# The order of four instructions in the projection stage of a two-layer recurrent and attention model

## The chip, the core and the metric

The kernel is written in Bass for one core of a Trainium2 chip. The metric is the device time of one execution in microseconds (us), lower being better. The engines are called as in the profile: PE is TensorE, DVE is VectorE, ACT is ScalarE, POOL is GpSimd, SP is SyncE, which here issues the transfers. Each engine takes its instructions strictly in the order written, and waits where the code says `wait_ge`.

## What is computed

Two layers over x of shape (4, 2048, 256). Each is `x + s * silu(g)` on a layernorm of x. In layer 0, s is a recurrent mix over time and g a feed-forward net. In layer 1, s is a latent attention with rotary parts, and g is a channel mix. The stage of interest makes all operands of layer 1's attention and its gate. Of the reference:

```python
xn = _layernorm(x)
c_q = x @ W_DQ;  Qc = c_q @ W_UQ;  Qr = rope(c_q @ W_QR)
c_kv = x @ W_DKV;  Kc = c_kv @ W_UK;  Kr = rope(x @ W_KR);  V = c_kv @ W_UV
# gate: mixes of every row with the row before it
xr = mu_r * x + (1.0 - mu_r) * x_prev
xk = mu_k * x + (1.0 - mu_k) * x_prev
r = sigmoid(xr @ W_r.T)
out = r * (square(relu(xk @ W_k.T)) @ W_v.T);  g = silu(out)
```

In both halves the x is the normalised xn.

## The kernel before

Four stages follow each other: layer0, layer1_projections, attention, layer1_output. Each is a block with a barrier at its end. The stage of interest, layer1_projections (from L924), walks over 16 chunks of 512 tokens (4 batches of 4 chunks). Products are made in float16, with every operand as a high part (the value rounded) and a low part (the rest), so most tensors are made in two steps: X_high, a copy with rounding, mostly on ACT, then X_low = X - X_high on DVE or POOL.

The order is written out by hand: each engine has a function `body(b, c, left)` that issues its instructions for chunk n, and semaphores count the steps. `left` is 4 in the first three batches and then 3, 2, 1, 0, so `left >= 1` holds for chunks 0 to 14, and `left >= 2` for chunks 0 to 13. Work for the chunks ahead is woven in. In the order of the code the body for chunk n is, for each engine:

- PE (L1499 on): latents (lat), keys of the gate (k), key rotary part (kr); with the latents qc (L1484) and the query rotary part; the transposes of chunk n+1 (L1477, wait for xhat); then, when relu and xr_low are there, the first half of the products of xr with w_r, kc (waits for qc_low), the second half, the values, and the gate's value products (L1546), which wait for kc_low and act_k. All go through four PSUM tensors, two banks each.
- ACT (L1289 on): qc_high (L1293); xn_of(n+1) (L1231 to L1245), which reads the transposes and has kc_high (L1297) in its middle; sigmoid of r (L1304); values (L1307); xk_high(n+1) (L1254); qr_high (L1312); xr_high(n+1) (L1260); the latents of n+1 (L1280); normalise(n+2) (L1225, four activations, waits for rstd(n+2)); relu of n+1 (L1284); gate_sig (L1321).
- DVE (L1418 on): latents' low part, two key products with cosine and sine (L1430), qc_low (L1433), two query products (L1437), the layernorm statistics of n+2 (L1333), kc_low (L1442), aggregate(n+2) (L1340), xn_low(n+1) (L1345), mix(n+1) (L1354, xk and then xr), xk_low(n+1) (L1359), qr_low (L1452), gate_in (L1457).
- POOL (L1176 on): the key sum k_cos + k_sin (L1180); the square of relu (L1183); kr_high, a cast of 8x512 (L1186); the query sum (L1188); kr_low (L1190); rstd_of(n+2) (L1157 to L1162, four small instructions, waits for the aggregate of n+2); xr_low_of(n+1) (L1166, waits for xr_high of n+1); the gate product (L1198, waits for gate_sig).
- SP stores qc, kr, kc, qr, values and gate of each chunk, and loads rows four chunks ahead.

Of the kernel before, what the change touches and what calls it, by code (L numbers as in the profile page):

```python
# [10 lines left out]
ACT = mybir.ActivationFunctionType  # L11
# [8 lines left out]
TPC = CH // P  # L20
# [900 lines left out]
STORES = 5  # L921


def layer1_projections(nc, a, d, ident, rows_out, early, scales, first):  # L924
# [6 lines left out]
    with ExitStack() as ctx:  # L931
# [10 lines left out]
        relu = sb("b_relu", [P, KT, CH])  # L942
# [23 lines left out]
        scale = sb("b_scale", [P, ATTN + 1])  # L966
# [22 lines left out]
        k_cos = sb("b_kcos", [D_R, CH])  # L989
# [4 lines left out]
        kr = sb("b_kr", [D_R, 2, 2, CH], F16)  # L994
# [5 lines left out]
        ps_b = ctx.enter_context(nc.psum_tensor("b_ps1", [P, 2, CH], F32))  # L1000
# [7 lines left out]
        stored = [sem(f"b_stored{i}") for i in range(2)]  # L1008
# [8 lines left out]
        stats_done = sem("b_stats_done")  # L1017
# [16 lines left out]
        k_mm = sem("b_k_mm")  # L1034
# [6 lines left out]
        relu_done = sem("b_relu_done")  # L1041
# [6 lines left out]
        kr_sum = sem("b_kr_sum")  # L1048
        kr_high = sem("b_kr_high")
# [36 lines left out]
        def count(b, c):  # L1086

            return b * CPB + c

        def turns(b, c):  # L1090

            return b * (CPB // 2) + c // 2

        with nc.Block() as block:  # L1094
# [47 lines left out]
            @block.gpsimd  # L1142
            def _(pool):
                for counts_from_one in (kr_low, gate_done):
                    pool.sem_inc(counts_from_one, 1)
                pool.memset(half[:], -0.5).then_inc(consts_set, 1)
                pool.memset(zero_col[:], 0.0).then_inc(consts_set, 1)
                pool.memset(ones[:], 1.0).then_inc(consts_set, 1)
                pool.memset(eps[:], LN_EPS).then_inc(consts_set, 1)
                pool.memset(zeros[:], 0.0).then_inc(consts_set, 1)  # L1150
                pool.wait_ge(consts_set, 5)

                def rstd_of(n):

                    pool.wait_ge(mv_done, TPC * n + TPC)
                    pool.wait_ge(xhat_done, TPC * n)
                    nc.gpsimd.tensor_tensor(var_eps[:], mv[:, :, 1], eps[:], ALU.add).then_inc(rstd_done, 1)  # L1157
                    nc.gpsimd.tensor_tensor(shift[:], zeros[:], mv[:, :, 0], ALU.subtract).then_inc(rstd_done, 1)
                    pool.wait_ge(rstd_done, 4 * n + 2)
                    nc.gpsimd.tensor_tensor(rstd[:], var_eps[:], half[:], ALU.pow).then_inc(rstd_done, 1)  # L1160
                    pool.wait_ge(rstd_done, 4 * n + 3)
                    nc.gpsimd.tensor_tensor(shift[:], shift[:], rstd[:], ALU.mult).then_inc(rstd_done, 1)  # L1162

                def xr_low_of(n):
                    pool.wait_ge(xr_high, n + 1)
                    nc.gpsimd.tensor_tensor(xr_half[:, 1], x_r[:], xr_half[:, 0], ALU.subtract).then_inc(xr_low, 1)  # L1166

                rstd_of(0)
                rstd_of(1)
                xr_low_of(0)  # L1170
                pool.memset(val[:], 0.0).then_inc(consts_set, 1)
                pool.wait_ge(consts_set, 6)
                for s in range(2):
                    pool.memset(val[:, s].rearrange("p g j h e -> p (g j h) e")[:, :, D_H:D_H + 1], 1.0).then_inc(consts_set, 1)

                def body(b, c, left):  # L1176
                    n, s = count(b, c), c % 2

                    pool.wait_ge(kr_parts, 2 * n + 2)
                    nc.gpsimd.tensor_tensor(k_cos[:], k_cos[:], k_sin[:], ALU.add).then_inc(kr_sum, 1)  # L1180

                    pool.wait_ge(relu_done, n + 1)
                    nc.gpsimd.tensor_tensor(act_k[:], relu[:], relu[:], ALU.mult).then_inc(act_done, 1)  # L1183
                    pool.wait_ge(kr_sum, n + 1)
                    pool.wait_ge(stored[s], 16 * STORES * turns(b, c) + 16)
                    nc.gpsimd.tensor_copy(kr[:, s, 0, :], k_cos[:]).then_inc(kr_high, 1)  # L1186
                    pool.wait_ge(qr_parts, 2 * n + 2)
                    nc.gpsimd.tensor_tensor(q_cos[:], q_cos[:], q_sin[:], ALU.add).then_inc(qr_sum, 1)  # L1188
                    pool.wait_ge(kr_high, n + 1)
                    nc.gpsimd.tensor_tensor(kr[:, s, 1, :], k_cos[:], kr[:, s, 0, :], ALU.subtract).then_inc(kr_low, 1)  # L1190
                    if left >= 2:
                        rstd_of(n + 2)
                    if left >= 1:
                        xr_low_of(n + 1)

                        pool.wait_ge(gate_sig_done, n + 1)
                        pool.wait_ge(rows_out.stored[s], 16 * (NCH // 2 + turns(b, c)) + 16)
                        nc.gpsimd.tensor_tensor(gate[s][:], gate_in[:], gate_sig[:], ALU.mult).then_inc(gate_done, 1)  # L1198

                chunks(pool, body)  # L1200

            @block.scalar
            def _(act):
# [75 lines left out]
                        act.wait_ge(lat_mm, 2 * n + i + 1)  # L1279
                        nc.scalar.activation(lat[:, i], ps_a[:, i, :], ACT.Copy, scale=f).then_inc(lat_high, 1)  # L1280

                def mixed_keys(n):
                    act.wait_ge(k_mm, n + 1)
                    nc.scalar.activation(relu[:], ps_b[:], ACT.Relu, scale=mix_k_factor).then_inc(relu_done, 1)  # L1284

                latents_high(0)
                mixed_keys(0)

                def body(b, c, left):  # L1289
                    n, s = count(b, c), c % 2  # L1290
                    act.wait_ge(stored[s], 16 * STORES * turns(b, c) + 16)
                    act.wait_ge(qc_mm, n + 1)
                    nc.scalar.activation(qc[:, s, 0], ps_c[:], ACT.Copy, scale=q_factor).then_inc(qc_high, 1)  # L1293

                    def keys_high():
                        act.wait_ge(kc_mm, n + 1)
                        nc.scalar.activation(kc[:, s, 0], ps_c[:], ACT.Copy, scale=k_factor).then_inc(kc_high, 1)  # L1297

                    if left >= 1:
                        xn_of(n + 1, c + 1, keys_high)  # L1300
                    else:
                        keys_high()
                    act.wait_ge(r_mm, n + 1)
                    nc.scalar.activation(sig_r[:], ps_r, ACT.Sigmoid, scale=r_factor).then_inc(sig_done, 1)  # L1304
                    act.wait_ge(val_mm, n + 1)
                    act.wait_ge(consts_set, 8)
                    nc.scalar.activation(val[:, s, :, :, :, 0:D_H].rearrange("p g j h e -> p g (j h) e"),  # L1307
                                         ps_val.rearrange("p j (g h e) -> p g j h e", g=GROUPS, h=GH), ACT.Copy, scale=v_factor).then_inc(val_done, 1)
                    if left >= 1:
                        xk_high_of(n + 1)  # L1310
                    act.wait_ge(qr_sum, n + 1)
                    nc.scalar.activation(qr[:, s, 0, :], q_cos[:], ACT.Copy).then_inc(qr_high, 1)  # L1312
                    if left >= 1:
                        xr_high_of(n + 1)
                        latents_high(n + 1)
                    if left >= 2:
                        normalise(n + 2, c + 2)
                    if left >= 1:
                        mixed_keys(n + 1)
                    act.wait_ge(gate_in_done, n + 1 + 1)  # L1320
                    nc.scalar.activation(gate_sig[:], gate_in[:], ACT.Sigmoid).then_inc(gate_sig_done, 1)  # L1321

# [3 lines left out]
            def _(dve):  # L1326
# [8 lines left out]
                def aggregate(n):  # L1335

                    if n:
                        dve.wait_ge(rstd_done, 4 * n - 2)
                    for j in range(TPC):
                        nc.vector.bn_aggr(mv[:, j, :], stats[:, j, :]).then_inc(mv_done, 1)  # L1340
# [16 lines left out]
                def xk_low_of(n):  # L1357
                    dve.wait_ge(xk_high, n + 1)
                    nc.vector.tensor_tensor(xk_half[:, 1], x_k[:], xk_half[:, 0], ALU.subtract).then_inc(xk_low, 1)  # L1359
# [58 lines left out]
                def body(b, c, left):  # L1418
# [20 lines left out]
                    if left >= 2:  # L1439
# [1 line left out]
                    dve.wait_ge(kc_high, n + 1)  # L1441
                    nc.vector.scalar_tensor_tensor(kc[:, s, 1], ps_c[:], factor[:, WUK:WUK + 1], kc[:, s, 0],  # L1442
                                                   ALU.mult, ALU.subtract).then_inc(kc_low, 1)
                    if left >= 2:
                        dve.wait_ge(stats_done, TPC * (n + 2) + TPC)
                        aggregate(n + 2)
                    if left >= 1:
                        xn_low_of(n + 1)
                        mix(n + 1, c + 1)
                        xk_low_of(n + 1)  # L1450
                    dve.wait_ge(qr_high, n + 1)
                    nc.vector.tensor_tensor(qr[:, s, 1, :], q_cos[:], qr[:, s, 0, :], ALU.subtract).then_inc(qr_low, 1)  # L1452

# [637 lines left out]
```

## Time and profile before

| | us |
|---|---|
| median of 3 executions | 3606.49 |
| lowest, highest | 2026.82, 8032.47 |
| profiled execution | 2026.82 |
| its span, first to last instruction | 2025.1 |
| layer0, from 0 to 638.8 | 638.8 |
| layer1_projections, to 950.2 | 311.4 |
| attention, to 1962 | 1011.8 |
| layer1_output, to the end | 63.1 |

The profile is of one execution. A row of a timeline has the start in us from the span's start, the length, engine and line, the operation, output and inputs, and, after x, how many instructions it merges. In square brackets stands how long the engine was idle before it and what ended that. Of instructions that follow each other directly, the next may start up to 0.1 us before the end of the one before, so the distance of two starts (here called a slot) is what one costs.

### The profile page before, as it was taken

The page shows a single profiled execution, that of the slowest core. Times are in us where ns is not written, and L with a number is a line of the kernel's source. Part 1 is how long each engine was busy: PE and PEld are TensorE (multiplying, and loading weights), DVE is VectorE, ACT ScalarE, POOL GpSimd, SP SyncE. Part 2 cuts the span into 40 slices and gives each one's busy share as a digit, 9 for nine tenths or more (in the row PEclk, how much of TensorE's full clock was granted, in tenths as well). Part 3 has the DMA queues.
Part 4 walks back from the last instruction along what each step waited for, and adds up shares of the span by engine and source line. Part 5 has one row for each costly group of instructions (what it writes and reads, how often), then busy time and mean ns, then how long its engine had stood idle before and what let it go on. Part 6 is the DMA issues. An engine that isn't in the chain of part 4 may idle for free. (4 is left out here: it accounts for less than half of the span.)

```text
span 2025.1 us, 53401 instructions
## 1 busy us (share of the span) xinstructions
PE 1900.1 (94%) x22950; PEld 978.9 (48%) x22950; DVE 1729.8 (85%) x2249; ACT 1727.0 (85%) x2153; POOL 547.4 (27%) x426
## 2 busy tenths in 40 slices
PE   3999999999995999998999999999999999999986
PEld 1565565655653566664444443444434444344445
DVE  5999999999987788886888888888888888888878
ACT  5767867777666888886999999999999999999972
POOL 0564554655644666764000000000000000000004
PEclk9999999999997999998999999999999999999999
DMA  3001001001112356567221222222222222122129
GB/s 108 22 22 42 22 22 42 22 22 42 54 42 78 129 191 204 190 170 210 70 75 55 67 68 74 73 55 68 68 74 72 62 62 55 51 62 60 56 96 329
DMA packets 130220, 166.24 MB, mean 82 GB/s; under 512 B 13632, under 2 KB 101696, under 8 KB 129728
## 3 DMA queue, kind: packets, MB, share of 16 engines
q1 hardware_dynamic: 127952, 160.59, 26.5%
q8 instruction: 180, 2.95, 0.6%
q10 hardware_dynamic: 2032, 2.24, 0.3%
q14 instruction: 56, 0.46, 0.1%
HBM read 91.21 MB, written 71.57 MB: 80 GB/s over the span
## 5 line engine op out<-in xcount | busy, mean ns | idle before, releaser
L1757 ACT ACTIVATE c_probs<-c_ps_b 128x1536 f32<-128x1536 f32 x544 | 891.9, 1640 | 0.0
L1871 PE MATMUL c_ps_o<-c_probs,c_v 128*32 128x256 f32 (+3 forms) x6656 | 582.3, 453 | 3.9 <-DVE c_probs L1789 0.8
L1789 DVE TENSOR_SCALAR c_probs<-c_probs 128x2048 f32<-128x2048 f32 (+2 forms) x415 | 433.7, 1055 | 68.2 <-ACT c_probs L1757 67.8
L1851 PE MATMUL c_ps_b<-c_qk 24*128 24x256 f16 (+2 forms) x8064 | 459.9, 294 | 5.7 <-PEq L1094 5.7
L1851 PE MATMUL c_ps_a<-c_qk 24*128 24x256 f16 (+2 forms) x2688 | 449.9, 294 | 6.5 <-ACT c_probs L1756 4.9
L1756 ACT ACTIVATE c_probs<-c_ps_a 128x512 f32<-128x512 f32 x544 | 422.9, 777 | 2.5 <-PE c_ps_a L1851 2.4
L1851 PEld LDWEIGHTS c_ps_b<-c_qk 24*128 24x128 f16 x8064 | 222.8, 93 | 332.6 <-ACT c_probs L1757 243.9
L2022 POOL TENSOR_TENSOR d_prod<-d_prod,d_x 128x1024 f32<-128x1024 f32 x4 | 13.1, 3262 | 1029.4 <-DVE d_prod L2011 1029.4
L1871 PEld LDWEIGHTS c_ps_o<-c_probs,c_v 128*32 128x32 f32 x6656 | 161.7, 109 | 245.8 <-issue 126.9
L278 POOL TENSOR_TENSOR a_hidh<-a_hid,a_hidh 128x512 f16<-128x512 f32 x128 | 207.2, 1648 | 135.2 <-ACT a_hidh L404 134.0
L1794 DVE TENSOR_SCALAR c_probs<-c_probs 128x1536 f32<-128x1536 f32 (+2 forms) x208 | 165.6, 803 | 55.9 <-ACT c_probs L1757 53.6
L1851 PEld LDWEIGHTS c_ps_a<-c_qk 24*128 24x128 f16 x2688 | 199.3, 93 | 18.0 <-ACT c_probs L1756 15.3
L728 PE MATMUL a_ps<-a_xnh,a_w 128*128 128x512 f16 x768 | 176.2, 381 | 12.8 <-ACT a_hid L399 12.0
L728 PE MATMUL a_ps<-a_w,a_hidh 128*128 128x256 f16 x1536 | 170.8, 273 | 1.5 <-POOL a_hidh L278 1.5
L1798 DVE SCALAR_TENSOR_TENSOR c_probs<-c_probs,c_caps 128x512 f32<-128x512 f32 x256 | 169.5, 682 | 0.0
L728 PEld LDWEIGHTS a_ps<-a_w,a_hidh 128*128 128x128 f16 x1536 | 149.9, 98 | 23.3 <-POOL a_hidh L278 2.4
L728 PEld LDWEIGHTS a_ps<-a_xnh,a_w 128*128 128x128 f16 x768 | 72.1, 97 | 114.2 <-ACT a_hid L399 29.0
L399 ACT ACTIVATE a_hid<-a_ps,a_b 128x512 f32<-128x512 f32 x128 | 87.9, 687 | 20.2 <-PE a_ps L728 15.1
L728 PE MATMUL a_ps<-a_xnh,a_wr 128*128 128x512 f16 x384 | 87.1, 383 | 10.3 <-DVE a_wv L525 10.3
L477 ACT ACTIVATE a_rwkvh<-a_rwkv 128x1024 f16<-128x1024 f32 x16 | 16.9, 1057 | 79.1 <-DVE a_rwkv L693 79.1
L515 DVE TENSOR_TENSOR a_xmixh<-a_xmix,a_xmixh 128x1024 f16<-128x1024 f32 x32 | 77.3, 2453 | 0.0
L1764 DVE STREAM_TRANSPOSE c_otok<-c_ps_o 128x512 f32<-128x512 f32 x64 | 45.8, 716 | 35.2 <-PE c_ps_o L1871 35.2
(272 smaller groups left out, 2776.9 us busy)
## 6 DMA issues: line engine op xcount, KB each, us to landing
v_d<-b_val SPq DMA_DIRECT2D x16, 1024.0 KB
c_v<-v_d SPq DMA_DIRECT2D x64, 256.0 KB
rows<-in_x SPq DMA_DIRECT2D x16, 512.0 KB, 4.9
x_d<-rows_out SPq DMA_DIRECT2D x16, 512.0 KB, 3.3
rows<-x_d SPq DMA_DIRECT2D x16, 512.0 KB, 5.0
qc_d<-b_qc SPq DMA_DIRECT2D x16, 512.0 KB
kc_d<-b_kc SPq DMA_DIRECT2D x16, 512.0 KB
gate_d<-rows_out SPq DMA_DIRECT2D x16, 512.0 KB, 3.3
```

The costliest lines, as they stand in the source:

```text
L278: nc.gpsimd.tensor_tensor(hid_half[:, 1, m], hid[:, m % RING], hid_half[:, 0, m], ALU.subtract).then_inc(hid_low, 1)
L399: nc.scalar.activation(hid[:, m % RING, :], ps_a[:, m % 2, :], ACT.Relu, bias=b_1[:, m:m + 1], scale=hid_scale).then_inc(hid_done, 1)
L515: nc.vector.tensor_tensor(x_mix_half[i][:, 1], x_mix[m][:], x_mix_half[i][:, 0], ALU.subtract).then_inc(mix_low, 1)
L728: mm = nc.tensor.matmul(ps, l, r, start=(first and i == 0), stop=(last and i == len(steps) - 1))
L1756: nc.scalar.activation(probs[:, t % NPROB, PARTS[0]], ps_a[:], ACT.Exp, scale=unscale).then_inc(exp_a_done, 1)
L1757: nc.scalar.activation(probs[:, t % NPROB, PARTS[1]], ps_b[:, t % 2], ACT.Exp, scale=unscale).then_inc(exp_b_done, 1)
L1764: nc.vector.transpose(o_tok[:, e % 2].rearrange("p k r -> p (k r)"), ps_o[:]).then_inc(tok_done, 1)
L1789: nc.vector.tensor_scalar(tile, tile, P_MAX, P_MIN, ALU.min, ALU.max).then_inc(clip_done, 1)
L1794: nc.vector.tensor_scalar(tile[:, :, at:end], tile[:, :, at:end], P_MAX, P_MIN, ALU.min, ALU.max)
L1798: op = nc.vector.scalar_tensor_tensor(tile[:, :, at:at + P], tile[:, :, at:at + P], P_MIN, cap, ALU.max, ALU.min)
L1851: mm = nc.tensor.matmul(into, k[rows, hk, kt * P:(kt + 1) * P], tokens[rows, hq], start=(i == 0), stop=(i == len(TERMS) - 1), tile_positio ...
L1871: mm = nc.tensor.matmul(ps_o[j * VW:(j + 1) * VW, column:column + w], v[:, kt, j * VW:(j + 1) * VW], probs[:, step % NPROB, j, at:at + w], ...
```

## The change

It moves four instructions or groups within `layer1_projections`, all inside the bodies above. On POOL the cast kr_high goes away, and xr_low_of(n+1) is put in front of rstd_of(n+2) where it was behind it. On ACT the same cast is made as an ACTIVATE between xn_of(n+1) and the sigmoid of r, and the relu, which stood before gate_sig at the end of the body of the chunk before, is the first instruction of its own chunk's body, and so comes right behind gate_sig. On DVE aggregate(n+2) goes from before xn_low(n+1) to behind xk_low(n+1).

```diff
--- before.py
+++ after.py
@@ -1181,17 +1181,15 @@
 
                     pool.wait_ge(relu_done, n + 1)
                     nc.gpsimd.tensor_tensor(act_k[:], relu[:], relu[:], ALU.mult).then_inc(act_done, 1)
-                    pool.wait_ge(kr_sum, n + 1)
-                    pool.wait_ge(stored[s], 16 * STORES * turns(b, c) + 16)
-                    nc.gpsimd.tensor_copy(kr[:, s, 0, :], k_cos[:]).then_inc(kr_high, 1)
                     pool.wait_ge(qr_parts, 2 * n + 2)
                     nc.gpsimd.tensor_tensor(q_cos[:], q_cos[:], q_sin[:], ALU.add).then_inc(qr_sum, 1)
                     pool.wait_ge(kr_high, n + 1)
                     nc.gpsimd.tensor_tensor(kr[:, s, 1, :], k_cos[:], kr[:, s, 0, :], ALU.subtract).then_inc(kr_low, 1)
+                    if left >= 1:
+                        xr_low_of(n + 1)
                     if left >= 2:
                         rstd_of(n + 2)
                     if left >= 1:
-                        xr_low_of(n + 1)
 
                         pool.wait_ge(gate_sig_done, n + 1)
                         pool.wait_ge(rows_out.stored[s], 16 * (NCH // 2 + turns(b, c)) + 16)
@@ -1279,15 +1277,12 @@
                         act.wait_ge(lat_mm, 2 * n + i + 1)
                         nc.scalar.activation(lat[:, i], ps_a[:, i, :], ACT.Copy, scale=f).then_inc(lat_high, 1)
 
-                def mixed_keys(n):
+                latents_high(0)
+
+                def body(b, c, left):
+                    n, s = count(b, c), c % 2
                     act.wait_ge(k_mm, n + 1)
                     nc.scalar.activation(relu[:], ps_b[:], ACT.Relu, scale=mix_k_factor).then_inc(relu_done, 1)
-
-                latents_high(0)
-                mixed_keys(0)
-
-                def body(b, c, left):
-                    n, s = count(b, c), c % 2
                     act.wait_ge(stored[s], 16 * STORES * turns(b, c) + 16)
                     act.wait_ge(qc_mm, n + 1)
                     nc.scalar.activation(qc[:, s, 0], ps_c[:], ACT.Copy, scale=q_factor).then_inc(qc_high, 1)
@@ -1300,6 +1295,8 @@
                         xn_of(n + 1, c + 1, keys_high)
                     else:
                         keys_high()
+                    act.wait_ge(kr_sum, n + 1)
+                    nc.scalar.activation(kr[:, s, 0, :], k_cos[:], ACT.Copy).then_inc(kr_high, 1)
                     act.wait_ge(r_mm, n + 1)
                     nc.scalar.activation(sig_r[:], ps_r, ACT.Sigmoid, scale=r_factor).then_inc(sig_done, 1)
                     act.wait_ge(val_mm, n + 1)
@@ -1315,8 +1312,6 @@
                         latents_high(n + 1)
                     if left >= 2:
                         normalise(n + 2, c + 2)
-                    if left >= 1:
-                        mixed_keys(n + 1)
                     act.wait_ge(gate_in_done, n + 1 + 1)
                     nc.scalar.activation(gate_sig[:], gate_in[:], ACT.Sigmoid).then_inc(gate_sig_done, 1)
 
@@ -1441,13 +1436,13 @@
                     dve.wait_ge(kc_high, n + 1)
                     nc.vector.scalar_tensor_tensor(kc[:, s, 1], ps_c[:], factor[:, WUK:WUK + 1], kc[:, s, 0],
                                                    ALU.mult, ALU.subtract).then_inc(kc_low, 1)
-                    if left >= 2:
-                        dve.wait_ge(stats_done, TPC * (n + 2) + TPC)
-                        aggregate(n + 2)
                     if left >= 1:
                         xn_low_of(n + 1)
                         mix(n + 1, c + 1)
                         xk_low_of(n + 1)
+                    if left >= 2:
+                        dve.wait_ge(stats_done, TPC * (n + 2) + TPC)
+                        aggregate(n + 2)
                     dve.wait_ge(qr_high, n + 1)
                     nc.vector.tensor_tensor(qr[:, s, 1, :], q_cos[:], qr[:, s, 0, :], ALU.subtract).then_inc(qr_low, 1)
```

## Rows read from the trace of the kernel before

**Rows 1.** Windows: the stage; busy us (count) of PE, PEld, DVE, ACT, POOL; PE clock

```profile
638.80:950.20 311.40, 283.34 (x1570) 175.74 (x1570) 252.97 (x432) 247.47 (x356) 197.93 (x184) 0.96 0.60 189
```

**Rows 2.** Windows, same columns: one chunk, from one qc ACTIVATE to the next

```profile
756.79:774.61 17.82, 17.43 (x100) 10.88 (x99) 15.07 (x25) 14.83 (x21) 12.26 (x12) 1.00 0.59 192
```

**Rows 3.** Timeline of PE, 740 to 780: start, length, what [idle before <-releaser]

```profile
763.23 3.72 PE L1546 MATMUL b_ps<-b_wv,b_actk 128*128 128x256 f32 x16 [0.39 <-DVE b_kc L1442]
766.79 2.75 PE L1484 MATMUL b_ps<-b_xnh,b_wc 128*128 128x512 f16 x12
...
776.14 1.48 PE L1484 MATMUL b_ps<-b_wr,b_xrh 128*128 128x256 f16 x12
```

**Rows 4.** Waits of ten chunks, 703.35 to 881.50: us in total, times, longest

```profile
POOL b_xrh L1166 <- ACT b_xrh L1260: 21.8, 10, 2.2
```

**Rows 5.** Timeline of ACT, 755 to 780, columns as in rows 3

```profile
756.79 1.02 ACT L1293 ACTIVATE b_qc<-b_ps 128x1024 f16<-128x1024 f32 x1 [0.48 <-PE b_ps L1484]
...
760.83 1.02 ACT L1297 ACTIVATE b_kc<-b_ps 128x1024 f16<-128x1024 f32 x1
...
765.98 1.06 ACT L1254 ACTIVATE b_xkh<-b_xk 128x1024 f16<-128x1024 f32 x1 [1.14 <-DVE b_xk L1354]
766.94 0.61 ACT L1312 ACTIVATE b_qr<-b_qcos 128x512 f16<-128x512 f32 x1
767.46 1.04 ACT L1260 ACTIVATE b_xrh<-b_xr 128x1024 f16<-128x1024 f32 x1
...
770.07 2.06 ACT L1225 ACTIVATE b_xhat<-rows,b_shift,b_rstd 128x256 f32<-128x256 f32 x4
772.17 1.02 ACT L1284 ACTIVATE b_relu<-b_ps 128x1024 f32<-128x1024 f32 x1
773.09 1.05 ACT L1321 ACTIVATE b_gs<-b_gi 128x1024 f32<-128x1024 f32 x1
```

**Rows 6.** Timeline of DVE, 755 to 780

```profile
760.37 1.40 DVE L1333 BATCH_NORM_STATS2 b_stats<-rows 128x6 f32<-128x256 f32 x4
761.89 1.28 DVE L1442 SCALAR_TENSOR_TENSOR b_kc<-b_ps,b_factor,b_kc 128x1024 f16<-128x1024 f32 x1
763.09 0.37 DVE L1340 BATCH_NORM_AGGREGATE b_mv<-b_stats 128x2 f32<-128x6 f32 x4
763.38 1.25 DVE L1345 SCALAR_TENSOR_TENSOR b_xnh<-b_ps,b_scale,b_xnh 128x1024 f16<-128x1024 f32 x1
764.55 1.40 DVE L1354 SCALAR_TENSOR_TENSOR b_xk<-b_ps,b_mix_now,b_prev 128x512 f32<-128x512 f32 x2
```

**Rows 7.** Timeline of POOL, 755 to 780

```profile
764.68 0.19 POOL L1157 TENSOR_TENSOR b_var<-b_mv,b_eps 128x4 f32<-128x4 f32 x1
...
766.20 0.20 POOL L1162 TENSOR_TENSOR b_shift<-b_shift,b_rstd 128x4 f32<-128x4 f32 x1
768.58 2.41 POOL L1166 TENSOR_TENSOR b_xrh<-b_xr,b_xrh 128x1024 f16<-128x1024 f32 x1 [2.19 <-ACT b_xrh L1260]
```

**Rows 8.** Timeline of ACT, the last chunk

```profile
934.92 1.02 ACT L1293 ACTIVATE b_qc<-b_ps 128x1024 f16<-128x1024 f32 x1 [0.47 <-PE b_ps L1484]
938.40 1.02 ACT L1297 ACTIVATE b_kc<-b_ps 128x1024 f16<-128x1024 f32 x1 [2.45 <-PE b_ps L1484]
```

**Rows 9.** Timelines: xr_low before chunk 0, DVE idle; DVE's qr_low beside rows 7

```profile
661.01 2.13 POOL L1166 TENSOR_TENSOR b_xrh<-b_xr,b_xrh 128x1024 f16<-128x1024 f32 x1 [10.31 <-ACT b_xrh L1260]
768.31 0.68 DVE L1452 TENSOR_TENSOR b_qr<-b_qcos,b_qr 128x512 f16<-128x512 f32 x1
```

**Rows 10.** Timeline of ACT, chunk 0

```profile
667.72 1.02 ACT L1293 ACTIVATE b_qc<-b_ps 128x1024 f16<-128x1024 f32 x1 [1.41 <-PE b_ps L1484]
...
677.08 1.06 ACT L1254 ACTIVATE b_xkh<-b_xk 128x1024 f16<-128x1024 f32 x1
```

**Rows 11.** Timeline of PE, its first projection; windows in the output stage, columns as rows 1

```profile
657.35 5.28 PE L1484 MATMUL b_ps<-b_xnh,b_wc 128*128 128x512 f16 x12 [10.16 <-DVE b_xnh L1345]
...
2005.00:2010.00 5.00, 3.52 (x33) 2.92 (x32) 4.96 (x4) 1.06 (x1) 1.96 (x1) 1.00 1.08 379
```

## The prediction

> **What bounds the kernel now.** I read four views. The split by stages: layer1_projections is 311.40 of 2025.1 us and PE is busy in 283.34 of them [rows 1]; the change touches nothing else. The table of one chunk: one chunk takes 17.82 us and PE is busy in 17.43 of it [rows 2], so PE sets the pace. PE's timeline: its only idle time is 0.39 us before the key-value products, for kc_low [rows 3]. The waits: POOL waits about 2.2 us a chunk for xr_high before it can make xr_low [rows 4]. That wait costs nothing now, since what stands behind it on POOL (the gate product) is needed by nobody soon. ACT, DVE and POOL have slack, each in a certain place, and the change uses up one of these places.
>
> I count from T, the end of a chunk's qc ACTIVATE (756.79 + 1.02 = 757.81, [rows 5]); the next such end is now T + 17.82. The first and last chunks show the same activation at 667.72 and 934.92 [rows 8, 10]: 16 chunks, 15 steps.
>
> **The moves that cost nothing alone.** The 8x512 cast goes from POOL to ACT. No ACT row has 8 partitions; the nearest is the 128x512 copy, which takes a slot of 0.52 us (766.94 to 767.46, [rows 5]). From below it could cost about 0.2, as no row excludes a cheaper one; I take 0.52. It stands before sig_r, in front of ACT's idle 1.14 us before xk_high [rows 5], which hides it; without that cover it is 0.52 x 16 = 8.3 us. The swap of relu and gate_sig on ACT: both have about 0.92 us slots back to back, and qc waits after them for PE; relu ends 0.9 later, at 774.1, while PE reaches the products with w_r that need it at 776.14 [rows 3]. The removed POOL cast makes POOL earlier. On DVE the aggregate (slot 0.29, 763.09 to 763.38) goes behind xk_low, so mix comes 0.29 earlier [rows 6]. None of these shortens what PE waits for: kc_low stands before the moved instructions.
>
> **The move that costs.** rstd_of(n+2) stood before xr_low on POOL and ended at 766.40 [rows 7], 3.67 us before ACT's normalise at 770.07 [rows 5]. Now it stands behind xr_low(n+1), which waits for ACT's xr_high. Behind rstd on ACT wait normalise, gate_sig, then relu and qc of the next chunk; behind qc stand DVE's qc_low, PE's kc products and again the mix that xr_high waits for. So a loop closes from qc to qc through three engines:
>
> - T to kc_low. ACT's xnh no longer waits for PE, which has its transposes done long before. PE's kc products wait for qc_low, as in the last chunk, where kc_high starts 938.40 - 935.94 = 2.46 after qc's end [rows 8] and so ends at 3.48. DVE has the statistics up to 761.77, T + 3.96, less the 0.08 by which DVE's instructions overlap: kc_low starts at 3.88 (now 4.08).
> - kc_low to mix: 1.20 to the next start, 1.17 from xn_low to xk (763.38 to 764.55), 1.40 for xk [rows 6]: 7.65, and 0.03 to ACT: xk_high at 7.68. ACT alone would be there at 764.84 - 757.81 = 7.03, less 0.56 for the earlier kc_high, plus 0.52 for the cast: 6.99. So 0.7 of cover is left for the cast.
> - xk_high, qr_high, xr_high: 765.98 to 768.50 = 2.52, now at 10.20. POOL starts 0.08 later: 10.28.
> - xr_low: 2.13 us with DVE idle, 2.41 when DVE's qr_low overlaps it by 0.41 [rows 7, 9]. Now qr_low, pushed by the aggregate, falls fully into it (xk_low, bound by mix, ends near 10.1, aggregate near 10.3, then 0.68 of qr_low). In proportion 0.28 / 0.41 x 0.66 = 0.45: I take 2.58, bounds 2.13 and 2.81 (all of qr_low added). End 12.86.
> - rstd's four instructions: 764.68 to 766.40 = 1.72, beginning 0.03 early [rows 7]: 14.55, and with 0.08 to ACT 14.63. ACT is ready near 12: it now stalls over 2 us.
> - normalise 2.10 (770.07 to 772.17), gate_sig 0.92, relu 0.92, qc 1.02 [rows 5]: 19.59.
>
> The loop is 19.59 us, longer than 17.82 by 1.77, and than PE's 17.43. PE's products are done before ACT wants them: today ACT gets qc's at 756.79 + 17.82 = 774.61, 16.80 after T, and all that PE does behind kc_low comes 0.2 earlier with it: 16.6, against ACT's 18.57. PE waits instead, 2.2 us in three pieces: for relu, qc_low and kc_low.
>
> On the rule of the lock: the row with 2.41 us shows POOL and DVE at work together, with 0.28 us lost of 0.41 shared [rows 7, 9]. The Trainium skill (SBUF — State Buffer, Who interferes with whom) says that a VectorE instruction with two SBUF inputs and a GpSimd one that reads SBUF lock each other out, and that the first to start wins. By it xr_low, starting just before qr_low, would keep 2.13 us and qr_low would wait; the sum would be 14 x 0.45 = 6 us smaller.
>
> **The sum.** rstd_of(n+2) exists in chunks 0 to 13: 14 steps. Chunk 0 has a table load on ACT, and there xk_high waits for nobody: it starts at 677.08, 8.34 after T [rows 10]; with the cast 8.86, and with 2.52 and the rest of the loop (19.59 - 10.20 = 9.39) it gives 20.77, or +2.95. Thirteen steps at +1.77 give 23.0. The step from chunk 14 to 15 has no rstd and gains about 0.2. Sum: 25.7. The profiled execution took 2026.8 us, 1.7 more than its span of 2025.1; the kernel after: 2052.5. The median shown, 3606.5, lies between one run of 2026.8 and one of 8032.5; nothing in this profile belongs to those two, so I go by the profiled one.
>
> **Rivals.**
> *Absorbed, no change.* If normalise starts less than 0.5 us late, the idle time of ACT before qc takes it. ACT starts it now at T + 12.26, and I have 14.63. For that, 1.9 us of xr_low and rstd (4.3 together) would have to vanish; no row has them shorter than 3.85. Or POOL would have to let rstd pass the waiting xr_low, against which speaks that nothing on POOL's timeline stands out of the order of the code. Time 2027; if even PE's kc_low wait went, 0.39 x 16 = 6 less, 2021. Chance 0.07.
> *The loop is longer than PE can follow (over 2%).* Other instructions on POOL or the handover cost more, and each late product delays the next: 42 us need 3.0 us a step, a loop of 20.8. The rows give at most 0.23 more for xr_low. Time 2070 to 2085, chance 0.05.
> *The clock falls.* PE gets gaps of up to about 1 us. At the stage's start, with the clock between its two levels, 12 products took 5.28 us, against 2.75 at the upper one [rows 3, 11]. So PE's chunk would take at least 17.43 x 5.28 / 2.75 = 33.5 us at 1.2 GHz, 15.6 more than now, and 14 of them give 2245. But in the output stage PE is busy for 3.52 of 5.00 us, less than the 89% here, with the clock at 1.00 [rows 11]. Chance 0.03. The Trainium skill (TensorE: The Clock Gate, A second HAM failure mode) describes many small gaps between groups of products that make the clock swing; this trace does not show it.
> *Only the size is off.* xr_low at 2.13 gives 2046, at 2.81 2056; handovers of 0.1 more at three places 2057. This is within the forecast.
>
> **How the numbers follow.** Forecast 0.85, with its own range 2043 to 2060. The range 2038 to 2062 adds the scatter of executions and leaves out the rivals, about 2 in 10 with misjudged sizes. Two per cent, about what a measurement of this kernel can tell from no change, is 40.5 us; 25.7 us are 1.3%. Slower by over 2% (the two slow rivals): 0.07. Faster: 0.02. Within: 0.91.
>
> **What would show it.** The distance of qc's ACTIVATEs 19.6 us in chunks 1 to 13 and 17.6 in the last; ACT idle about 2 us a chunk before the normalise, released by POOL's shift; xr_low 2.4 to 2.7 us; PE with 17.4 us busy per chunk at clock 1.00 and new waits for relu and for qc_low; the stage 337 us long; all other stages unchanged. ACT not idle before the normalise, or a distance of 17.8, would refute the loop; a clock under 1.00 in mid-stage would speak for the clock's rival.

## The result and the profile after

The changed kernel takes 2049.7 us (median of 4, 2048.3 to 2050.0). The kernel before takes 2026.7 us (median of 19 executions beside the first experiments, 2026.2 to 2027.6). Of 35 later executions of it, one was high like two of the first table, at 2393 us and a granted clock of 0.749 instead of 0.985; times compared here leave such executions out. The ratio of changed to before is 1.0114 (95% interval 1.0096 to 1.0133): 23 us, 1.1% slower, inside the two per cent and clear of the scatter.

The stages, in the windows view (busy us and count of PE, PEld, DVE, ACT, POOL; granted clock; DMA):

```profile
638.80:972.00 333.20, 288.25 (x1570) 173.72 (x1570) 251.21 (x432) 254.60 (x372) 193.04 (x165) 0.96 0.56 175
972.00:1984.00 1012.00, 994.53 (x17408) 414.53 (x17408) 851.50 (x1136) 1001.96 (x1091) 0.50 (x2) 0.99 0.24 63
1984.00:2047.60 63.60, 46.87 (x384) 38.82 (x384) 54.65 (x40) 15.35 (x15) 24.30 (x8) 0.90 0.95 330
```

The first window ends a little early: the first instruction of the attention starts at 972.74, at 950.19 before. So the projection stage has grown by 22.5 us. From PE's first product of the attention to the end of the span it is 1074.8 us now and 1074.9 before. PE has the same 1570 products in the stage.

One chunk now, first as a window from one qc ACTIVATE to the next, then ACT's timeline in the same chunk (start, length, what, idle before and its releaser):

```profile
765.96:785.45 19.49, 17.77 (x98) 10.74 (x98) 14.95 (x24) 15.31 (x23) 11.99 (x11) 1.00 0.54 176
```

```profile
765.96 1.00 ACT L1288 ACTIVATE b_qc<-b_ps 128x1024 f16<-128x1024 f32 x1
...
771.48 0.61 ACT L1299 ACTIVATE b_kr<-b_kcos 8x512 f16<-8x512 f32 x1
...
774.64 1.06 ACT L1252 ACTIVATE b_xkh<-b_xk 128x1024 f16<-128x1024 f32 x1 [0.74 <-DVE b_xk L1349]
775.60 0.61 ACT L1309 ACTIVATE b_qr<-b_qcos 128x512 f16<-128x512 f32 x1
776.12 1.04 ACT L1258 ACTIVATE b_xrh<-b_xr 128x1024 f16<-128x1024 f32 x1
...
781.62 2.07 ACT L1223 ACTIVATE b_xhat<-rows,b_shift,b_rstd 128x256 f32<-128x256 f32 x4 [2.53 <-POOL b_shift L1162]
783.60 1.04 ACT L1316 ACTIVATE b_gs<-b_gi 128x1024 f32<-128x1024 f32 x1
784.55 1.00 ACT L1285 ACTIVATE b_relu<-b_ps 128x1024 f32<-128x1024 f32 x1
785.45 1.00 ACT L1288 ACTIVATE b_qc<-b_ps 128x1024 f16<-128x1024 f32 x1
```

The distance of two qc is 19.49 us where it was 17.82 [rows 2, 5]. ACT, which waited for POOL in none of these chunks before, now idles 2.53 us before the normalise until POOL's shift arrives. From there it works without a pause through qc. POOL and DVE at the same place:

```profile
777.24 2.67 POOL L1166 TENSOR_TENSOR b_xrh<-b_xr,b_xrh 128x1024 f16<-128x1024 f32 x1 [3.92 <-ACT b_xrh L1258]
779.87 0.20 POOL L1157 TENSOR_TENSOR b_var<-b_mv,b_eps 128x4 f32<-128x4 f32 x1
...
781.39 0.20 POOL L1162 TENSOR_TENSOR b_shift<-b_shift,b_rstd 128x4 f32<-128x4 f32 x1
```

```profile
770.83 1.26 DVE L1437 SCALAR_TENSOR_TENSOR b_kc<-b_ps,b_factor,b_kc 128x1024 f16<-128x1024 f32 x1
...
776.97 0.37 DVE L1335 BATCH_NORM_AGGREGATE b_mv<-b_stats 128x2 f32<-128x6 f32 x4
777.26 0.66 DVE L1447 TENSOR_TENSOR b_qr<-b_qcos,b_qr 128x512 f16<-128x512 f32 x1
```

The aggregate has been there since 777.34; rstd starts at 779.87, directly behind xr_low. So it is the order on POOL that holds it, not its input. PE shows where this ends, with three waits a chunk in place of one [rows 3]:

```profile
766.12 1.49 PE L1479 MATMUL b_ps<-b_wr,b_xrh 128*128 128x256 f16 x12 [0.39 <-ACT b_relu L1285]
768.34 1.04 PE L1479 MATMUL b_ps<-b_lat,b_wuk 128*128 128x512 f16 x4 [0.74 <-DVE b_qc L1428]
...
772.15 3.72 PE L1541 MATMUL b_ps<-b_wv,b_actk 128*128 128x256 f32 x16 [0.59 <-DVE b_kc L1437]
```

Together they are 1.72 us instead of 0.39. The clock is 1.00 in this chunk as before.

The distances of the 16 qc ACTIVATEs, read off ACT's timelines: before 17.80 to 17.82 in all 15 steps; after 20.57, then thirteen times 19.49 or 19.50, then 17.22. From first to last that is 291.23 us in place of 267.20 [rows 8, 10].

### The profile page after: what moved, and what is told of

Same layout as the page of the kernel before. It is cut to its first block and busy times, and to the rows that moved or that the text cites. A ratio compares the mean times of both kernels' runs of the same rounds, so it can differ in the third digit from the quotient of the medians.

```text
span 2047.6 us, 53385 instructions
## 1 busy us (share of the span) xinstructions
PE 1905.1 (93%) x22950; PEld 976.5 (48%) x22950; DVE 1728.6 (84%) x2249; ACT 1734.4 (85%) x2169; POOL 542.7 (27%) x410
```

## The experiments

The theory is a loop: ACT's qc; DVE's qc_low, query products, statistics, kc_low, xn_low and mix; ACT's xk_high, qr_high and xr_high; POOL's xr_low and rstd; ACT's normalise, gate_sig, relu and again qc. The rivals are that the loss comes from the other moved instructions, or that ACT's wait is a sign and not the cause. Each run was timed beside the kernel before. A step is the distance of two qc ACTIVATEs.

### Undo the order on POOL alone

```diff
-                    if left >= 1:
-                        xr_low_of(n + 1)
                     if left >= 2:
                         rstd_of(n + 2)
                     if left >= 1:
+                        xr_low_of(n + 1)
```

> The changed kernel with one part undone: POOL does rstd_of(n+2) before xr_low_of(n+1) again; cast, relu and aggregate stay where the change put them. Theory (a loop through POOL, in which rstd waits behind xr_low): the loop opens. The aggregate ends about 10.5 us after qc's end, rstd 1.7 us later at 12.3, where ACT is ready for the normalise at 12.3 (it is held there by the latents); at most 0.1 us is late, and ACT has 0.5 us of idle time before qc. The distance of two qc goes back from 19.49 to 17.82, the time to 2026 to 2028 us, as before the change. Rival (the cast on ACT, or the aggregate behind xk_low, costs the time): the distance stays above 18.5 and the time above 2038 us.

2025.8 us (10 executions), ratio 0.9995 (0.9985 to 1.0005): the whole loss is gone, with cast, aggregate and relu still moved. The steps are 18.47, 17.57 and then 17.80 to 17.82. ACT in this kernel:

```profile
771.18 2.08 ACT L1222 ACTIVATE b_xhat<-rows,b_shift,b_rstd 128x256 f32<-128x256 f32 x4 [0.44 <-POOL b_shift L1162]
773.16 1.04 ACT L1315 ACTIVATE b_gs<-b_gi 128x1024 f32<-128x1024 f32 x1
774.11 1.00 ACT L1284 ACTIVATE b_relu<-b_ps 128x1024 f32<-128x1024 f32 x1
775.18 1.02 ACT L1287 ACTIVATE b_qc<-b_ps 128x1024 f16<-128x1024 f32 x1
```

ACT still waits for POOL here, 0.44 us and not the 0.1 that was expected (rstd's first instruction took 0.55 us instead of 0.19 in this place, beside DVE's qr_low). The chunk has room for it: the wait is visible in the view, and the steps are those of the kernel before.

### The order on POOL alone, from the kernel before

```diff
-                    if left >= 2:
-                        rstd_of(n + 2)
                     if left >= 1:
                         xr_low_of(n + 1)
-
+                    if left >= 2:
+                        rstd_of(n + 2)
+                    if left >= 1:
```

> The kernel before with one part of the change alone: on POOL xr_low_of(n+1) before rstd_of(n+2). Theory: the whole loss appears, a little more than in the changed kernel since the aggregate's 0.29 us stays in the loop, while xr_low shares 0.43 us instead of 0.66 us with qr_low. Loop: 3.88 + 1.20 + 0.29 + 1.17 + 1.40 + 0.03 = 7.97, + 2.52 + 0.08 + 2.42 (xr_low) + 1.69 + 0.08 + 2.10 + 0.92 + 0.92 + 1.02 = 19.72; less 0.10, by which the changed kernel was shorter than worked out in the same way: 19.6 us. Time 2048 to 2054 us. Rival (the parts share the loss, or they act only together): under 2040 us.

2049.8 us, ratio 1.0114 (1.0097 to 1.0131), steps 19.82, then 19.49 to 19.51, last 17.22. One move makes the whole loss. The steady step is even the same as with all moves. Here the aggregate's slot of 0.29 us is in the loop, and xr_low shares less time with qr_low:

```profile
757.78 2.41 POOL L1166 TENSOR_TENSOR b_xrh<-b_xr,b_xrh 128x1024 f16<-128x1024 f32 x1 [3.05 <-ACT b_xrh L1261]
```

It takes 2.41 us, in the changed kernel 2.67. So the aggregate's move took 0.29 us out of the loop and put 0.26 us back, by pushing qr_low beside xr_low.

### The cast alone

```diff
 # POOL
-                    pool.wait_ge(kr_sum, n + 1)
-                    pool.wait_ge(stored[s], 16 * STORES * turns(b, c) + 16)
-                    nc.gpsimd.tensor_copy(kr[:, s, 0, :], k_cos[:]).then_inc(kr_high, 1)
 # ACT, between xn_of and the sigmoid of r
+                    act.wait_ge(kr_sum, n + 1)
+                    nc.scalar.activation(kr[:, s, 0, :], k_cos[:], ACT.Copy).then_inc(kr_high, 1)
```

> The kernel before with another part alone: the 8x512 cast made by ACT between xn_of and the sigmoid of r, not by POOL. Theory: it takes a slot of 0.52 us and is hidden in ACT's idle 1.14 us before xk_high, which falls to 0.6; the distance of two qc stays 17.82, the time is within 1 us of before, about 2026 us. Rival (the cast is on ACT's path): 16 x 0.52 = 8 us more, 2034 us.

2026.0 us (10 executions), ratio 0.9997 (0.9987 to 1.0006), steps 17.81 to 17.84.

```profile
762.15 0.61 ACT L1301 ACTIVATE b_kr<-b_kcos 8x512 f16<-8x512 f32 x1
762.67 1.00 ACT L1303 ACTIVATE b_sigr<-b_ps 128x1024 f32<-128x1024 f32 x1
...
765.25 1.06 ACT L1251 ACTIVATE b_xkh<-b_xk 128x1024 f16<-128x1024 f32 x1 [0.69 <-DVE b_xk L1353]
```

The cast takes a slot of 0.52 us, as the nearest row of a copy said, and ACT's idle time before xk_high falls from 1.14 to 0.69.

### How much cover there is: five casts

The kernel of the last section with four more casts, into a tile `extra` that nobody reads (its declaration is left out):

```diff
                     nc.scalar.activation(kr[:, s, 0, :], k_cos[:], ACT.Copy).then_inc(kr_high, 1)
+                    for i in range(4):
+                        nc.scalar.activation(extra[:, i], k_cos[:], ACT.Copy)
```

> The kernel before with the cast on ACT five times, four of them into a tile that nobody reads, 2.6 us of ACT a chunk in place of 0.52. It measures how much cover stands before xk_high. Theory: ACT is ready for xk_high 7.03 us after qc's end, with the casts at 9.63; xk_high 1.06, xk_low 1.25, products with w_k 2.7, with w_kr 1.4, with w_q 1.14, qc 1.02 end at 18.24 against 17.82: 15 x 0.42 = 6 us more, 2033 us. So of 2.6 us only 0.4 show. Rival (ACT is on the path): 15 x 2.6 = 39 us, 2065 us. Rival (the slack is larger than I see): 2026 us.

2037.8 us, ratio 1.0055 (1.0040 to 1.0071), steps 19.90 and then 18.47 or 18.48. The cover is limited, as the theory says, but the expected 18.24 was too low, because the wrong wait was taken for the next one. PE:

```profile
767.04 3.72 PE L1548 MATMUL b_ps<-b_wv,b_actk 128*128 128x256 f32 x16 [0.39 <-DVE b_kc L1444]
771.25 2.76 PE L1486 MATMUL b_ps<-b_xnh,b_wc 128*128 128x512 f16 x12 [0.48 <-ACT b_val L1309]
773.85 2.75 PE L1486 MATMUL b_ps<-b_xkh,b_wk 128*128 128x512 f16 x12
```

PE's latents wait for ACT's copy of the values, which frees their PSUM banks. It stands ahead of xk_high on ACT, and its slack had not been counted: it ends 9.56 us after qc's end, PE goes on at 9.62, and with its products (2.60, 2.68, 1.40), 1.15 to ACT and 1.02 for qc the loop is 18.47.

### qr_low away from xr_low

From the changed kernel (queries_low is qr_low with its wait, as a function; its definition is left out):

```diff
                 def body(b, c, left):
 # behind the latents' low part
+                    if n:
+                        queries_low(n - 1, 1 - s)
 # before q_cos and q_sin are written again
+                    if n:
+                        dve.wait_ge(qr_low, n)
 # behind aggregate(n + 2)
-                    dve.wait_ge(qr_high, n + 1)
-                    nc.vector.tensor_tensor(qr[:, s, 1, :], q_cos[:], qr[:, s, 0, :], ALU.subtract).then_inc(qr_low, 1)
+                    if left == 0:
+                        queries_low(n, s)
```

> The changed kernel with DVE's qr_low(n) moved behind the latents' low part of the next chunk, so that it no longer runs beside POOL's xr_low. Theory (the two share a way into SBUF): xr_low falls from 2.67 to 2.13 us as in the row with DVE idle, the distance of two qc from 19.49 to about 18.95, the time by 13 x 0.54 = 7 us to about 2042 us. Rival (xr_low's length has another cause, such as ACT or PE at work beside it): xr_low stays at 2.67 us and the time at 2049 us.

One execution, 2042.9 us; steps 20.12, then thirteen of 18.96 or 18.97, last 17.22. All of xr_low:

```profile
L1166 POOL TENSOR_TENSOR b_xrh<-b_xr,b_xrh x16: 2128/2137/2140, 661.1 to 945.4; 128x1024 f16<-128x1024 f32 x16
```

Minimum, median and maximum are now 2128, 2137 and 2140 ns; in the changed kernel the median is 2666. The 0.53 us saved on POOL show as 0.53 us in the distance of two qc. That is the loop measured by a dose: what xr_low gives, every chunk gives.

### gate_sig before the normalise

```diff
-                    if left >= 2:
-                        normalise(n + 2, c + 2)
                     act.wait_ge(gate_in_done, n + 1 + 1)
                     nc.scalar.activation(gate_sig[:], gate_in[:], ACT.Sigmoid).then_inc(gate_sig_done, 1)
+                    if left >= 2:
+                        normalise(n + 2, c + 2)
```

> The changed kernel with ACT's gate_sig(n) put before normalise(n+2) instead of behind it. Its input is there 12.1 us after qc's end, when ACT begins to wait for rstd. Theory (everything on ACT between rstd's arrival and qc is in the loop): gate_sig's slot of 0.95 us leaves the loop, the distance of two qc falls from 19.49 to 18.55, ACT's idle time before the normalise from 2.53 to about 1.6, the time by 13.5 x 0.95 = 13 us to 2037 us. Rival (ACT's idle time is only a sign of something that paces the chunks elsewhere): 19.49 and 2049.7 us stay.

2036.8 us, ratio 1.0051 (1.0036 to 1.0067), steps 19.62, then 18.54 to 18.56, last 17.22.

```profile
758.30 2.08 ACT L1223 ACTIVATE b_xhat<-rows,b_shift,b_rstd 128x256 f32<-128x256 f32 x4 [1.48 <-POOL b_shift L1162]
760.28 1.00 ACT L1285 ACTIVATE b_relu<-b_ps 128x1024 f32<-128x1024 f32 x1
761.19 1.01 ACT L1288 ACTIVATE b_qc<-b_ps 128x1024 f16<-128x1024 f32 x1
```

About two fifths of ACT's idle time (2.53 us) are filled, 1.48 are left, and the step is shorter by 0.94, the slot of gate_sig. The work is the same and only its order differs, so ACT's wait is no mere sign: it sets the step.

### gate_sig and relu before the normalise

```diff
                     act.wait_ge(gate_in_done, n + 1 + 1)
                     nc.scalar.activation(gate_sig[:], gate_in[:], ACT.Sigmoid).then_inc(gate_sig_done, 1)
+                    if left >= 1:
+                        mixed_keys(n + 1)
+                    if left >= 2:
+                        normalise(n + 2, c + 2)
```

(mixed_keys is the relu again as a function, called once ahead of the loop; the two lines of the normalise are taken from in front, as above.)

> The changed kernel with gate_sig(n) and relu(n+1) both before normalise(n+2) on ACT. Theory: relu waits for PE's products with w_k, 14.1 us after qc's end, and ends its slot at 15.0, 0.35 us behind rstd's arrival at 14.66. Then come the normalise (2.0) and qc (1.02): 18.0 instead of 19.49. So most of the loss goes although POOL's order stays as changed: 14 x 1.49 = 21 us less, about 2029 us. Rival (the order on POOL costs by itself, wherever ACT's work stands): above 2040 us.

2028.4 us, ratio 1.0010 (1.0001 to 1.0020), steps 18.72, then 18.01 or 18.02 as expected, last 17.43. ACT:

```profile
770.25 1.06 ACT L1318 ACTIVATE b_gs<-b_gi 128x1024 f32<-128x1024 f32 x1
772.25 1.02 ACT L1284 ACTIVATE b_relu<-b_ps 128x1024 f32<-128x1024 f32 x1 [0.94 <-PE b_ps L1485]
773.17 2.06 ACT L1223 ACTIVATE b_xhat<-rows,b_shift,b_rstd 128x256 f32<-128x256 f32 x4
775.13 1.00 ACT L1292 ACTIVATE b_qc<-b_ps 128x1024 f16<-128x1024 f32 x1
```

rstd is in time again, since relu's wait for PE now covers it. POOL's order is still the changed one, and nine tenths of the loss are gone.

### A faster kernel, from the kernel before

```diff
 # ACT, xn_of: kc_high behind the first prev, not the second
-                        if i and between:
-                            between()
+                            if i and k == 0 and between:
+                                between()
 # PE: kc in the middle of the second of four token tiles of w_r, not behind it
-                        if j == TPC // 2:
+                            if j == 1 and i == len(steps) // 2:
 # DVE: statistics of tiles 0, 1 before kc_low, of 2, 3 behind it
-                        layernorm(n + 2, c + 2, b + (c + 2) // XS)
+                        layernorm(n + 2, c + 2, b + (c + 2) // XS, (0, 1))
```

> A try at a faster kernel, from the kernel before. PE's one wait, 0.39 us a chunk for kc_low, is to go: PE makes the kc products after one and a half of the four token tiles of w_r instead of two, ACT makes kc_high after the first and not the second prev, and DVE makes two of the four statistics behind kc_low. Theory (PE's work is the bound): kc_high starts about 0.5 us earlier, kc_low ends before PE's values do, the distance falls from 17.82 to 17.45, the time by 16 x 0.38 = 6 us to about 2020.5 us. Rival (another wait takes its place, such as xk_low): 2026 us.

2019.6 us (2019.2 to 2020.1), ratio 0.9966 (0.9954 to 0.9979): the fastest of all. A stretch of 17 us, a little less than a chunk (columns as in rows 1):

```profile
753.30:770.30 17.00, 17.00 (x99) 10.69 (x97) 14.81 (x25) 14.47 (x21) 11.92 (x12) 1.00 0.62 201
```

PE is busy all the time. The steps are 17.48 and then 17.34 or 17.35, less than the 17.45 expected: besides the 0.39 of PE's wait another 0.08 went, since the products before the wait, 1.04 us long, have a slot of 0.96 where the next follow at once. With PE's products as they are, no order of the other engines can make these chunks shorter.

## The prediction, step by step

**Right: the place and the mechanism.** The loop exists, through the instructions named, in the chunks named, and it is made by the one move named as costly. One link was too many: PE's kc products are named in the loop, but kc_high ends before DVE is through with the statistics, so DVE's own order leads to kc_low, as the forecast's terms have it. The terms, in us after qc's end (766.96 in the rows shown, 785.45 + 1.00 the next), read off the timelines above:

| | forecast | measured |
|---|---|---|
| kc_low starts | 3.88 | 3.87 |
| xk_high starts | 7.68 | 7.68 |
| xr_low starts | 10.28 | 10.28 |
| xr_low's length | 2.58 | 2.67 |
| rstd ends | 14.55 | 14.63 |
| normalise starts | 14.63 | 14.66 |
| qc ends: the step | 19.59 | 19.49 |
| step from chunk 0 | 20.77 | 20.57 |
| last step | 17.6 | 17.22 |

**Mis-sized terms.** The sum was +25.7 and the time came out 2.8 us lower than 2052.5. Of the span's +22.5, the 15 steps give +24.0 and the time before the first qc -0.3. The rest, -1.2, is a term that the forecast put at nothing.
- the end of the stage (forecast 0, measured -1.2). From the last qc to PE's first product of the attention it was 15.31 us and is 14.14. In the last chunk kr_low ends 6.23 us after the start of qc and not 7.92, and behind kr_low stand SP's last four stores of operands. The DMA share is the last column but one in these windows, up to the next stage, of the kernel before and then of the changed one:

```profile
947.00:950.20 3.20, 0.00 (x0) 0.00 (x0) 1.12 (x1) 0.00 (x0) 0.01 (x1) 0.85 1.01 366
970.72:972.74 2.02, 0.00 (x0) 0.00 (x0) 1.12 (x1) 0.00 (x0) 0.00 (x1) 1.00 0.24 89
```

  The swap on POOL alone leaves this end as it was (15.32); the cast alone makes it 14.70, and all moves but the swap make it 14.14. So it is a gain of the moves called costless. That the stores carry it is argued from these windows, not tested.
- normalise to the next instruction: taken as 2.10 from two starts, measured 1.98. In [rows 5] the normalise ends at 772.13 and relu, which starts at 772.17, needs PE's products with w_k; the 2.10 had a short wait in it. Over 14 steps this is 1.7 us, the largest term. A slot should be read where nothing can wait.
- xr_low 0.09 longer than the proportion gave; POOL to ACT took 0.03, not 0.08. With 0.01 less for rstd these leave +0.03.
- the last step: the forecast left the statistics in it. Chunk 14 has none, so kc_low waits for kc_high alone and starts 0.4 earlier.
- PE's waits were put at 2.2 us, as the step less 17.43. They are 1.72: a PE that stops and starts shows more busy time for the same products, 17.77 (the first products with w_r show 1.49 us with a pause behind them, while before, where the next follow at once, their slot is 1.31).

**The lock.** The forecast read the 2.41 us of [rows 7] as two engines at work together, 0.28 lost of 0.41 shared, and scaled this to 0.45 for 0.66. The value was near, the form wrong. The runs fit a wait, in which POOL gets the shared time less 0.13 on top: 0.28 for 0.41, and 0.53 for 0.66, which makes 2.66 of the 2.67 measured. So POOL waits for nearly all of qr_low, as by an exclusive lock. The forecast's sentence on that rule lets xr_low, which the record has first by 0.02 us, keep its 2.13; but it was xr_low that waited. The last section has the rows.

**The step that failed: what a measurement can tell.** The text put two per cent as "about what a measurement of this kernel can tell from no change", with no row behind it, and so filed +25.7 us as "within", at 0.91. The runs showed ten times finer: the 19 executions beside the first experiments lie within 1.4 us (0.07%), and the ratio's interval is 0.2% to either side, 1.0096 to 1.0133. So a slowdown that is clear of the scatter was forecast as one that could not be told. With a forecast of +1.3% and an own range of 2043 to 2060, the statement that followed was that the change makes the kernel slower, clearly and by under two per cent. The mechanism was right; besides this step, what was off is the sizes above: the end of the stage (nothing, measured -1.2), the normalise (2.10, measured 1.98) and the last step (17.6, measured 17.22). For the time before, the forecast went by the one profiled execution and not by the median shown, and the later executions at 2026.7 bore this out.

**The rivals.** Absorbed: it would have needed 1.9 us less on POOL; the undo on POOL shows how it looks when it holds (0.44 late, steps of 17.8). Over two per cent: no further wait was found. The clock: granted 1.00 from 700 us to the end of the stage in spite of three gaps of 0.39 to 0.74 us a chunk. Beside the rival's price a row was misread: over the 5.28 us of the first products [rows 11] the granted clock was 0.51, the lower level and not between the two, so 33.5 us is the price and not the least of it. The Trainium skill's case of many small gaps that make the clock swing (TensorE: Matmul & The Clock Gate, A second HAM failure mode: psum-queue depth-cycling) did not come up in this stage.

**Costless moves.** The cast is shown to cost nothing (its own run), and all three together as well (the undo on POOL); both gain a little at the stage's end, as said above. That the relu's and the aggregate's moves cost nothing each by itself was not run.

## What to carry to other kernels

Before a short instruction is put behind one that waits on an in-order engine, ask who waits for it and whether the long wait's own source comes from that reader: then a queue order closes a loop, and no busy share shows it, since here no engine got more than the 0.5 us of a cast to do and all of them got idle time. The end of the stage is no turn of the loop and has to be priced by itself; here it gave 1.2 us back. Walk the loop once from an instruction back to itself in slots; its length against the bound engine's step is the price per turn. If a late value can't come earlier, put independent work of the waiting engine in front of the wait: two such moves brought back 21 of 23 us here.

## What the runs showed of the hardware

Long instructions of DVE and POOL that each read two operands in SBUF take turns here. POOL's 128x1024 subtraction takes 2.13 us alone, 2.31 beside 0.31 us of such a DVE subtraction (the kernel with five casts), 2.41 beside 0.41 us, 2.58 beside 0.58 us (the changed kernel, chunk 0) and 2.67 beside 0.66 us. Each is 2.13 plus the time shared less 0.13, while DVE's instruction keeps its 0.66 to 0.69 us. In layer 0 of the kernel before it is DVE that pays. Its 128x1024 subtraction, first two of them with POOL idle, then one by one, and POOL's instructions beside them:

```profile
28.16 2.35 DVE L515 TENSOR_TENSOR a_xmixh<-a_xmix,a_xmixh 128x1024 f16<-128x1024 f32 x2
...
108.34 1.16 POOL L278 TENSOR_TENSOR a_hidh<-a_hid,a_hidh 128x512 f16<-128x512 f32 x1
108.81 1.77 DVE L515 TENSOR_TENSOR a_xmixh<-a_xmix,a_xmixh 128x1024 f16<-128x1024 f32 x1
109.46 3.33 POOL L284 TENSOR_TENSOR a_on<-a_on,a_sigr 128x1024 f32<-128x1024 f32 x1
110.50 3.37 DVE L515 TENSOR_TENSOR a_xmixh<-a_xmix,a_xmixh 128x1024 f16<-128x1024 f32 x1
```

DVE's takes 1.21 us alone, 1.77 with 0.69 us shared behind POOL's subtraction and 3.37 with 2.29 us shared behind POOL's product: 1.21 + 0.69 - 0.13 and 1.21 + 2.29 - 0.13. POOL's product takes 2.36 where it comes first (at 72.44) and 3.33 here, behind 1.12 us of the DVE instruction from 108.81: 2.36 + 1.12 - 0.13 is 3.35. So whichever comes second waits until the other has ended. The Trainium skill (SBUF — State Buffer, Who interferes with whom) calls this an exclusive lock, and the trace agrees. What the start in the record does not tell is who has it when two starts nearly coincide: in the changed kernel xr_low starts at 777.24 and qr_low at 777.26, and it is xr_low that waits. With POOL first by 0.47 us or more, POOL had it. That the lock is taken some time after the recorded start, and by POOL later than by DVE, would fit both, but was not tested.
